# Eleven blocks of values per half, two bursts behind their scores, with the heads turned behind a block

## The reference

```
xn = layernorm(x)
q, k = rope(xn @ wq + bq), rope(xn @ wk + bk);  v = xn @ wv + bv
s = softmax(q k^T / sqrt(16)) v                      # 32 heads, 1024 x 1024 scores each
z = xn @ W^T + b;  m = sum_e p_e (xn A_e) B_e
gamma = min(0.5 * |z| / (|m| + 1e-6), 1)
out = x + s * silu(z + gamma * m)
```

## Time and profile before

| | before |
|---|---|
| time, median of 3 runs | 525.4 us (524.22 to 529.4) |
| profiled execution, time | 528.23 us |
| its span | 526.4 us |
| mean granted clock of TensorE in it | 0.912 |
| busy: PE, DVE, ACT, POOL | 94%, 70%, 58%, 17% |

### The profile page before, as it was taken

How to read it: one execution, slowest core, us unless ns; L and a number is a source line. 1 busy time by engine, 2 the same in 40 slices (tenths; PEclk the granted TensorE clock), 3 DMA queues, 4 the chain that set the end, 5 groups by cost and what they waited for, 6 DMA issues and landing times.

```text
span 526.4 us, 8762 instructions
## 1 busy us (share of the span) xinstructions
PE 493.2 (94%) x3237; PEld 215.3 (41%) x3237; DVE 371.1 (70%) x401; ACT 303.4 (58%) x593; POOL 88.3 (17%) x159
## 2 busy tenths in 40 slices
PE   7897999999999999999999999999999999999996
PEld 3572444433443434343434334343434344343332
DVE  6543888887868878787878777787878787244401
ACT  2210002366767767676867666677777686654652
POOL 8551114430010010001000100100010001015421
PEclk9997999996988989898989987898989898999857
DMA  9899644440000000000000000000000000010000
GB/s 271 256 129 127 90 60 60 65 58 2 1 1 2 2 1 1 2 1 2 0 2 2 1 2 0 2 1 1 1 2 1 2 0 2 2 72 17 19 27 27
DMA packets 13360, 17.42 MB, mean 33 GB/s; under 512 B 3088, under 2 KB 7440, under 8 KB 13328
## 3 DMA queue, kind: packets, MB, share of 16 engines
q1 hardware_dynamic: 11808, 15.84, 16.1%
q10 hardware_dynamic: 1520, 1.12, 0.8%
HBM read 6.72 MB, written 2.10 MB: 17 GB/s over the span
## 4 chain that ended last, share of the span: by engine, by line
PE 68%; DVE 14%; issue 7%; SPq 4%; DMA 3%; ACT 3%; POOL 0%; DVEq 0%; ACTq 0%
PE oT L882 25%; PE st L928 22%; DVE negmax L634 12%; PE sm L819 8%; PE st L759 5%; PE sm L901 3%; PE sm L892 3%; ACT arena L565 2%; SPq L311 2%; DMA kA<-arena 2%; PE oT L759 1%; DMA idb_sb<-in_identb 1%; PE sm L904 1%; SPq L279 1%; SPq L285 1%
## 5 line engine op out<-in xcount | busy, mean ns | idle before, releaser
L634 DVE TENSOR_REDUCE negmax<-sm 128x1 f32<-128x1024 f32 x256 | 300.9, 1220 | 79.9 <-PE sm L819 78.5
L565 ACT ACTIVATE arena<-st 128x512 f32<-128x512 f32 x512 | 269.5, 599 | 124.9 <-PE st L928 122.0
L819 PE MATMUL sm<-kA,qA 48*128 48x512 f32 x512 | 193.7, 462 | 11.9 <-DVE negmax L634 6.6
L928 PE MATMUL st<-qA,kA 50*128 50x512 f32 x512 | 182.5, 457 | 2.7 <-ACT arena L565 1.3
L882 PE MATMUL oT<-arena,vg 128*32 128x256 f32 (+3 forms) x1792 | 163.9, 469 | 0.0
L928 PEld LDWEIGHTS st<-qA,kA 50*128 50x128 f32 x512 | 89.5, 198 | 122.7 <-ACT arena L565 79.6
L819 PEld LDWEIGHTS sm<-kA,qA 48*128 48x128 f32 x512 | 86.6, 195 | 50.2 <-DVE negmax L634 35.1
L882 PEld LDWEIGHTS oT<-arena,vg 128*32 128x32 f32 x1792 | 43.1, 115 | 63.0 <-issue 38.0
L404 POOL TENSOR_TENSOR maxp<-negmax,consts 128x16 bf16<-128x16 f32 x16 | 3.4, 214 | 259.2 <-DVE negmax L634 259.2
L492 ACT ACTIVATE arena<-arena 128x512 fp32r<-128x512 f32 x10 | 6.3, 630 | 58.0 <-POOL arena L367 58.0
L892 PE MATMUL sm<-id_sb,wkv 128*128 128x128 f32 x64 | 15.1, 380 | 10.1 <-DVE negmax L634 9.3
(11 more groups left out here) (88 smaller groups left out, 245.7 us busy)
## 6 DMA issues: line engine op xcount, KB each, us to landing
qA<-arena SPq DMA_DIRECT2D x48, 128.0 KB, 5.1
x_sb<-in_x SPq DMA_DIRECT2D x8, 256.0 KB, 5.8
kA<-arena SPq DMA_DIRECT2D x12, 128.0 KB, 6.7
wT_sb<-in_wT SPq DMA_DIRECT2D x1, 1024.0 KB, 9.2
out<-x_sb SPq DMA_DIRECT2D x1, 896.0 KB, 4.0
out<-x_sb SPq DMA_DIRECT2D x4, 224.0 KB, 1.9
z_sb<-in_wq SPq DMA_DIRECT2D x1, 768.0 KB, 10.1
wkv<-in_wk ACTq DMA_DIRECT2D x1, 256.0 KB, 4.3
```

The lines of the kernel that those rows point to most:

```text
L565: act.activation(probs[:, s % PB, h, :], st[:, (st_score(0, s, h) - late) % 3, :], ACT.Exp, scale=float(D) ** -0.5).then_inc(st_free, 1)
L634: dve.tensor_reduce(negmax[:, half, r:r + 1], sm[:, bank, :], AX.X, ALU.max, negate=True).then_inc(sm_free, 1)
L819: mm = pe.matmul(sm[:, bank, kh * HALF:(kh + 1) * HALF], qA[rows, half, g // 2, h, qt * P:(qt + 1) * P], kA[rows, g // 2, kh * HALF:(kh + ...
L928: pe.matmul(st[:, n % 3, :], kA[rows, g // 2, kt * P:(kt + 1) * P], qA[rows, half, g // 2, h, :], start=True, stop=True).then_inc(st_full, 1)
```

## The change

`LAG` becomes 2. The middle of a half is cut by key tiles in twos: each pair of key tiles (1 and 2, 3 and 4, 5 and 6) gives three blocks, of 384, of 128 + 256, and of 256 columns (`CUTS`). With blocks 0 and 10 of 512 columns there are 11 blocks, as many as bursts, so a block stands behind every burst. The block is issued ahead of the turn of the heads. The count of finished blocks that ACT and POOL wait for (`blocks_through`, `2 * BLOCKS`) follows. After the last burst of the kernel blocks 9 and 10 remain, where it was blocks 8 and 9. No instruction is added or removed on any engine.

```diff
-BURST, LAG = 3, 3
+BURST, LAG = 3, 2
-SPAN = 384
-BLOCKS = 2 + (NT - 2) * HALF // SPAN
+BLOCKS = 2 + 3 * (NT - 2) // 2
+CUTS = ((0, 0, 384), (0, 384, HALF), (1, 0, 256), (1, 256, HALF))
...
-    at, end = HALF + SPAN * (b - 1), HALF + SPAN * b
-    cut = min(end, (at // HALF + 1) * HALF)
-    return [(a // HALF, a % HALF, a % HALF + z - a) for a, z in ((at, cut), (cut, end)) if z > a]
+    two, third = (b - 1) // 3, (b - 1) % 3
+    return [(1 + 2 * two + kt, a, z) for kt, a, z in ((CUTS[0],), CUTS[1:3], CUTS[3:])[third]]
...
+                    if burst >= LAG:
+                        values(g, half, burst - LAG)
+                    elif half == 1:
+                        values(g, 0, burst - LAG + BLOCKS)
+                    elif not first:
+                        values(g - 1, 1, burst - LAG + BLOCKS)
                     if i == 4 * OUT1_SLOT - 1 and not first:
                         n = SM_LAST["out1"] if last else sm_out1(g)
                         turn_heads(1, n % 2, 2 * g, n - 1)
...
-                    b = (burst - LAG) % BURSTS
-                    if burst >= LAG:
-                        values(g, half, b)
-                    elif b < BLOCKS and half == 1:
-                        values(g, 0, b)
-                    elif b < BLOCKS and not first:
-                        values(g - 1, 1, b)
...
-            for b in range(BURSTS - LAG, BLOCKS):
+            for b in range(BLOCKS - LAG, BLOCKS):
```

More of the change, by code:

```diff
@@ L84 @@
 OUT1_SLOT, OUT0_SLOT = 3, 11
-BURST, LAG = 3, 3
+BURST, LAG = 3, 2
 BURSTS = -(-REP * NT // BURST)
-SPAN = 384
-BLOCKS = 2 + (NT - 2) * HALF // SPAN
+BLOCKS = 2 + 3 * (NT - 2) // 2
+CUTS = ((0, 0, 384), (0, 384, HALF), (1, 0, 256), (1, 256, HALF))
+assert BLOCKS == BURSTS
 def st_score(g, s, h):
@@ L110, in block_parts @@
         return [(0 if b == 0 else NT - 1, 0, HALF)]
-    at, end = HALF + SPAN * (b - 1), HALF + SPAN * b
-    cut = min(end, (at // HALF + 1) * HALF)
-    return [(a // HALF, a % HALF, a % HALF + z - a) for a, z in ((at, cut), (cut, end)) if z > a]
+    two, third = (b - 1) // 3, (b - 1) % 3
+    return [(1 + 2 * two + kt, a, z) for kt, a, z in ((CUTS[0],), CUTS[1:3], CUTS[3:])[third]]
 def blocks_through(g, s):
     kt = s % NT
-    return 2 * BLOCKS * g + BLOCKS * (s // NT) + (BLOCKS if kt == NT - 1 else 1 - (-kt * HALF // SPAN))
+    return 2 * BLOCKS * g + BLOCKS * (s // NT) + (1 + (3 * kt + 1) // 2 if kt < NT - 1 else BLOCKS)
 def sm_base(g):
```

## The result

| | before | changed |
|---|---|---|
| time, median of 4 runs each | 524.81 us | 495.14 us (494.34 to 497.1) |
| ratio of changed to before, 95% interval | | 0.943 (0.936 to 0.950) |
| profiled execution: time, span | 528.23, 526.4 us | 494.34, 492.5 us |
| its mean granted clock | 0.912 | 0.989 |

The account below looks back on a forecast made before the run. Bound: a PE-DVE loop with slack on both in the middle, the low clock in the last half. 528.2 - 14.2 (middle) - 10.9 (last half) + 0.1 = 503.2 us profiled; median forecast 501 us, range 494 to 512.

Parts of the forecast that it names:

- Clock in the middle: Middle halves: PE's clock stays at 2.4 GHz once each burst has its block; mean clock 0.912 to 0.97 or more.
- The hole: Start of a half: no block behind burst 2, PE waits for ACT and DVE, then 3.41 us at 1.2 GHz.
- The walk of DVE: DVE's work and waits through a middle half: 23.2 us against 24.24, bounds 22.8 and 23.6; 14.2 us saved in all.
- the row split by block 0: Fifth sm row of a half, split behind burst 2 by the block of 512: DVE waits 1.15 us.
- the small waits around the heads: DVE's small waits where the heads are turned in a half: 0.3 us.
- the row behind burst 4: sm row split behind burst 4 by a block of 384 columns: DVE waits 0.70 us.
- The row behind burst 0: sm row split behind burst 0 by a block of 256 columns: DVE waits 0.48 us.
- The other two: sm rows split behind bursts 6 (384 columns) and 8 (256 columns): DVE waits 0.70 and 0.48 us.
- Turn behind the block: Turn of the heads issued after block 1, which fills PE's wait of 0.72 us for DVE.
- The first half: Very first half of the kernel, where bursts 0 and 1 have no block in either kernel: 0.5 us saved.
- The last half: Second half of the last group, to the span's end: clock holds, 38.2 us becomes 27.3, 10.9 us less.
- The slower one: Rival: low clock lands on block 0 in a split row; 24.6 us per half, 531 us in all; chance 0.04.

Follow-up runs that it names:

- pair of kernels with repeated work: Kernel before and changed kernel, each with the st matmuls of bursts 2 and 3 of every half issued twice: 505.08 us and 504.11 us.
- filled-hole run: Kernel before with each st matmul of bursts 2 and 3 of every half issued twice, nothing moved: 505.08 us, ratio 0.976.
- LAG alone: Kernel before with only LAG set from 3 to 2, still ten blocks and the old order of turn and block: 519.42 us, ratio 0.999.
- turn first: Changed kernel with the turn of the heads put back ahead of the block: 495.31 us.
- LAG 3: Changed kernel with LAG put back from 2 to 3, still eleven blocks: 558.9 us, ratio 1.064.
- kernel filled in the last group only: Kernel before with the st matmuls of bursts 2 and 3 issued twice in the last group only: 517.43 us, ratio 0.991.
- bursts of two: Changed kernel with bursts of two pairs, sixteen blocks of 256 columns, LAG 3 and the last group's dense units moved: 479.49 us.

## Why the prediction was right, step by step

- **Clock in the middle.** Right, and by the pair of kernels with repeated work it is the gain there, but for 0.3 us per half at most. The mean clock went to 0.989 (forecast: 0.97 or more), with no low stretch between 138 and 410 us. The filled-hole run shows cause and not company: with nothing moved and work added, ten of 13 falls went and the time with them.
- **The hole.** Right in what it does, incomplete in what brings the clock down. A stretch in which PE was busy for 2.84 or 2.69 of 3.40 us stood before the falls shown of the kernel before and of LAG alone. But the same stretch stood in LAG alone without a fall, and one of 2.58 us with the turn first, so what decides between fall and no fall stays open, also why the traced run of before fell in all 13 middle halves. The wait ahead of the turn, which I counted to the hole, is innocent by itself (0.90 us with the turn first, no fall), while PE and ACT waiting for the copy with every block in place brings it down (LAG 3). That the copy would not hold ACT was right for LAG 2, and I had not seen how near it stood.
- **The walk of DVE.** The term for a half was mis-sized: 23.2 forecast, 22.64 measured, below my bound of 22.8. I had 1.15 for the row split by block 0, and it is 0.94, near the lower bound of 0.92. I had 0.3 for the small waits around the heads and 0.70 for the row behind burst 4, and they are 0.36 and 0.30. The row behind burst 0 takes 0.25 and not 0.48. The other two are as forecast, 0.70 and 0.48. These are 0.8 us too much, of which I had taken off 0.2 in going from 23.4 to 23.2; what is left is 0.56 us, and over 12 halves 6.7 us of the result. I had priced each wait by itself and added them, but where DVE starts late on one row the next row has been written meanwhile; that this is the reason fits the rows and was not tested. One price was read from the wrong row: the 0.89 for three pairs is that of three `st` alone, as the last half has no `sm`. Three pairs take 0.90 (210.71 to 211.61 in the trace of before), so nothing hangs on it.
- **Turn behind the block.** Forecast as filling 0.72 us of wait; the wait went and was worth nothing, since DVE had two rows in hand. The sum did not rest on it.
- **The first half.** 0.5 us forecast, 2.2 measured up to the first copy, which is in part luck. The low stretch that begins at 117 us lasted 3.41 us in the changed kernel's trace and 10.24 in that of before. But the kernel filled in the last group only has the order of before here, and there it lasted 6.83 us and the first copy came at 139.16, 1.3 us earlier than before. So 1.3 of the 2.2 us is what two runs of the same order differ by.
- **The last half.** 27.3 forecast, 27.0 measured; 1.68 us per burst forecast and measured; 5.5 us from the last copy to the end both times. That the clock would hold there was right. The reason given, that its own hole is what brings it down, is only half shown, and the kernel before itself may not fall there in its fastest runs.
- **The size.** 501 was forecast, 495.1 measured, inside 494 to 512 but 1.1 us from its edge. By the profiled runs I forecast 25.0 us of gain and measured 33.9. The two terms above, 6.7 and 1.7 us, make up nearly all of the 8.9 between them, the last half 0.3 more. All went the same way, and the half at 22.64 lies outside my own bounds for it; that the range held was luck to that extent.
- **The rivals.** The slower one does not occur in the changed kernel, but its mechanism was seen with LAG alone: low clock on block 0 inside a split row, 2.15 us of DVE. The rule of the Trainium skill ("TensorE: Matmul & The Clock Gate", section "A second HAM failure mode: psum-queue depth-cycling"), that brief idling between groups of matmuls makes the clock go back and forth, did not carry over to the short waits in the changed kernel: PE was idle for 9.45 of the 271.70 us of its middle, at a clock of 1.00. My row for it named DVE's busy time, which is not what that rule is about; PE was busy for 16.53 of those 17.00 us. In the kernel before and with LAG 3, where PE was idle for 0.56 and 1.57 of the 3.40 us ahead of a fall, the trace agrees.

## What to carry to other kernels

Look at the granted clock beside the timeline before pricing any reordering of PE: here a stretch in which PE had gaps, not a longer path, cost about 1.5 us in each middle half, and most of it went away by issuing the same matmuls twice. That is also the cheapest test of the cause: fill the hole with repeated work, and if the kernel gets faster, look for real work to put there. Take several runs and not one trace: the same hole let the clock fall in one half and not in the next. And when a block is moved later, look at what another engine has in its program order that waits for its end; with LAG 3, one copy behind the wrong exponential cost 58 us.

## What the runs showed of the hardware that was not expected

- The mean clock of one program differs from run to run: LAG alone ran in 512.5 to 529.2 us at mean clocks of 0.968 to 0.926. Kernels whose middle stays at full clock scatter too, from 0.2% (turn first, 494.76 to 495.62) to 1.8% (bursts of two, 477.5 to 486.3). The low stretch that begins near 117 us lasts 3.41 us in the trace of the changed kernel and 17.07 in that of the same kernel with repeated work:

```profile
117.50:134.57 17.07, 17.07 (x85) 6.99 (x83) 10.82 (x12) 9.35 (x19) 0.00 (x0) 0.50 0.01 2
```

- Once low, the clock came back after 3.41 us in 12 of the 13 middle halves of the kernel before (after 10.24 in one), and stayed low for 23.9 us in its last half with PE busy throughout. With full bursts in the same last half, the mean clock over 27.0 us was 0.99.
- 96 added matmuls of 512 columns cost the changed kernel 9 us by the medians and saved the kernel before 18.
